# Attention with a banded bias: ScalarE writes the bias of three heads of four into PSUM, and the probability product moves between two score units

## What is computed

```python
scores = einsum('bhid,bhjd->bhij', q, k) * scale
diag = i - j
in_band = (diag >= 0) & (diag < 256)
scores = scores + where(in_band, learnable_bias[:, clip(diag, 0, 255)], 0)
scores = where(diag >= 0, scores, -inf)
m = maximum(max(scores, -1), off)
p = exp(scores - m)
out = einsum('bhij,bhjd->bhid', p, v) / (sum(p, -1) + exp(off - m))
x = layernorm(x + out @ Wo.T)
```

## Time and profile before

| | |
|---|---|
| three runs | 1764.86, 1770.17, 1771.36 us; median 1770.17 |
| the profiled execution | 1767.04 us, span on the core 1765.2 us |
| PE busy | 1640.3 us, 93% of the span |
| DVE busy | 1280.5 us, 73% |
| ACT busy | 1087.4 us, 62% |
| POOL busy | 212.0 us, 12% |
| identity matmuls L684 | 1280, 352.3 us busy |
| seeds L940 and zeros L938 on ACT | 320 and 128, 197.1 and 70.0 us busy |
| mean granted TensorE clock | 0.965 of full speed |

### The profile page before, as it was taken

One profiled execution on the slowest core, in us unless ns is written; L12 is line 12 of the kernel. 1 busy time (PEld: TensorE's weight loads), 2 busy tenths in 40 slices (PEclk: granted clock), 3 DMA queues, 4 the chain that ended last, 5 costly groups with the idle time before them and its releaser, 6 DMA issues. The chain is left out here.

```text
span 1765.2 us, 27891 instructions
## 1 busy us (share of the span) xinstructions
PE 1640.3 (93%) x9158; PEld 764.5 (43%) x9168; DVE 1280.5 (73%) x3812; ACT 1087.4 (62%) x1576; POOL 212.0 (12%) x109
## 2 busy tenths in 40 slices
PE   7999899889999999999999999999999998878773
PEld 3444344334444444444444444444444444433331
DVE  2454667568788888878888888888888872777776
ACT  2333233237877888787788878788887886333332
POOL 4323323230000000000000000000000000222222
PEclk9999999989999999999999999999999999989795
DMA  5447363534533633543452443335334120112211
GB/s 213 143 152 214 135 179 126 143 120 79 104 49 63 121 49 49 111 72 49 97 85 50 85 77 70 81 64 87 81 54 72 39 85 4 61 56 72 72 44 52
DMA packets 124501, 156.97 MB, mean 89 GB/s; under 512 B 14915, under 2 KB 80515, under 8 KB 124102
## 3 DMA queue, kind: packets, MB, share of 16 engines
q1 hardware_dynamic: 124358, 155.19, 38.1%
HBM read 103.90 MB, written 50.46 MB: 87 GB/s over the span
## 5 line engine op out<-in xcount | busy, mean ns | idle before, releaser
L925 ACT ACTIVATE probs<-ps 128x1024 f32<-128x1024 f32 (+3 forms) x768 | 592.3, 810 | 178.3 <-PE ps L684 119.3
L1165 DVE CUSTOM_DVE_ANT_0 junk<-ps,bias_q 128x384 bf16<-128x384 f32 (+2 forms) x1024 | 501.5, 502 | 137.3 <-PE ps L657 126.3
L657 PE MATMUL ps<-k_stack,q_stack 96*128 96x384 bf16 (+3 forms) x1536 | 492.8, 334 | 19.3 <-DVE mx L1165 12.0
L678 PE MATMUL ps<-q_stack,k_stack 99*128 99x512 bf16 (+3 forms) x1536 | 489.8, 328 | 18.7 <-ACT ps L940 10.4
L1158 DVE TENSOR_REDUCE mx<-ps 128x1 f32<-128x128 f32 (+3 forms) x768 | 365.2, 485 | 44.8 <-PE ps L657 37.1
L750 PE MATMUL ps<-attn 128*128 128x512 f32 x768 | 351.7, 602 | 10.5 <-DMA attn<-hT 9.3
L684 PE MATMUL ps<-bias_r,ident_r 128*128 128x384 f32 (+2 forms) x1280 | 352.3, 363 | 0.0
L699 PE MATMUL ps<-probs,v_sb 128*32 128x512 f32 (+3 forms) x3072 | 327.3, 498 | 0.1
L657 PEld LDWEIGHTS ps<-k_stack,q_stack 96*128 96x128 bf16 x1536 | 142.5, 97 | 373.9 <-DVE mx L1165 136.8
L684 PEld LDWEIGHTS ps<-bias_r,ident_r 128*128 128x128 f32 x1280 | 222.2, 192 | 36.9
L750 PEld LDWEIGHTS ps<-attn 128*128 128x128 f32 x768 | 144.9, 193 | 176.1 <-issue 163.7
(11 more groups left out here) (103 smaller groups left out, 1004.1 us busy)
## 6 DMA issues: line engine op xcount, KB each, us to landing
q_stack<-q_parts SPq DMA_DIRECT2D x192, 128.0 KB, 4.3
v_dram<-v_sb SPq DMA_DIRECT2D x32, 512.0 KB, 2.8
v_sb<-v_dram SPq DMA_DIRECT2D x32, 512.0 KB, 9.8
k_stack<-k_parts SPq DMA_DIRECT2D x32, 384.0 KB, 7.3
q_parts<-q_stack SPq DMA_DIRECT2D x84, 128.0 KB, 2.0
k_parts<-k_stack SPq DMA_DIRECT2D x84, 128.0 KB, 2.0
attn<-hT SPq DMA_DIRECT2D x8, 1024.0 KB, 7.0
k_stack<-k_parts SPq DMA_DIRECT2D x32, 256.0 KB, 8.0
```

Of the source, the lines that this page charges most:

```text
L657: pe.matmul(ps_ring[:, use.bank, 0:c1 - c0], q_stack[0:STACK, b, hl, I * P:(I + 1) * P], k_stack[0:STACK, b, hl, c0:c1], start=True, stop= ...
L678: mm = pe.matmul(ps_s[:, u % 2, hh, 0:w], k_stack[0:ROWS, b, hl, J * P:(J + 1) * P], q_stack[0:ROWS, b, hl, i0:i0 + w], start=not in_bank, ...
L925: act.activation(probs[:, (u // 2) % 3, 2 * pr:2 * pr + 2, 0:w], ps_s[:, pr, :, 0:w], ACT.Exp).then_inc(exp_done, 1)
L1165: ins = dve.tensor_tensor_reduce(out=junk[:, use.bank, 0:c1 - lo], in0=ps_ring[:, use.bank, lo - c0:c1 - c0], in1=bias_q[:, hl, BAND - t0 ...
```

## The change

In the tiles with a bias ScalarE now seeds the bank of head 1 as well, and only head 0 gets its bias from the identity matmuls. So there is a seed after every unit whose tile has a successor with a band, not only after the odd units: after an even unit for one head, after an odd unit for two. Every score unit of such a tile waits for its own seed. In TensorE's order `pv(T-1)` moves from the end of unit 2T+1 to the end of unit 2T, between the two units of tile T; the last product of the batch before moves from unit 1 to unit 0. ScalarE's copies stay after units 1 and 9. GpSimd's split follows the heads.

```diff
-PV_LEFT, EVAC_LEFT, OT_LEFT = 1, 1, 4
+PV_LEFT, EVAC_LEFT, OT_LEFT = 0, 1, 4
...
-        bias_s = sb("bias_s", [P, 2, 2, BAND])
-        bias_r = sb("bias_r", [P, 2, 2, 2, BAND], FP32R)
+        bias_s = sb("bias_s", [P, 2, 3, BAND])
+        bias_r = sb("bias_r", [P, 2, 2, 1, BAND], FP32R)
...
-                in_bank = bw and u % 2
-                if in_bank:
-                    pe.wait_ge(seeded, n * NBAND + BANDED.index(u // 2) + 1)
+                if bw:
+                    pe.wait_ge(seeded, 2 * (n * NBAND + BANDED.index(u // 2)) + u % 2 + 1)
                 for hh in range(2):
                     hl = 2 * (u % 2) + hh
+                    in_bank = bw and hl
...
                         if left and u == PV_LEFT:
                             pv(*before_in(g, b), n - 1, NT - 1)
-                        if u % 2 and u > 1:
+                        if u % 2 == 0 and u:
                             pv(g, b, n, u // 2 - 1)
...
-            def seed(g, T, done=0):
+            def seed(g, u, done=0):
...
+                pr = u % 2
+                heads = slice(1 - pr, 2)
+                nh = 1 + pr
+                if u < 2:
                     act.wait_ge(bias_split, 3 * (g + 1))
                 act.wait_ge(exp_done, FIRST + done)
                 act.sem_inc(act_passed, 1)
                 if w > bw:
-                    act.activation(ps_s[:, 1, :, bw:w], zero[:, :].unsqueeze(2).broadcast_to([P, 2, w - bw]),
-                                   ACT.Copy)
-                act.activation(ps_s[:, 1:2, :, 0:bw], bias_s[:, bass.ds(g % 2, 1), :, b0:b0 + bw], ACT.Copy)\
+                    act.activation(ps_s[:, pr, heads, bw:w],
+                                   zero[:, 0:nh].unsqueeze(2).broadcast_to([P, nh, w - bw]), ACT.Copy)
+                act.activation(ps_s[:, pr:pr + 1, heads, 0:bw],
+                               bias_s[:, bass.ds(g % 2, 1), pr:1 + 2 * pr, b0:b0 + bw], ACT.Copy)\
                     .then_inc(seeded, 1)
 
             def seed_after(g, n, u, more):
-                if u % 2 and u + 2 < NU:
+                if u + 2 < NU:
                     if u // 2 + 1 in BANDED:
-                        seed(g, u // 2 + 1, n * NU + u + 1)
-                elif u % 2 and more:
-                    seed(*more, 0, n * NU + u + 1)
+                        seed(g, u + 2, n * NU + u + 1)
+                elif more:
+                    seed(*more, u % 2, n * NU + u + 1)
...
             seed(0, 0)
+            seed(0, 1)
...
-                pool.tensor_copy(hi, bias_in[:, 0:2, ::-1]).then_inc(bias_split, 1)
+                pool.tensor_copy(hi, bias_in[:, 0:1, ::-1]).then_inc(bias_split, 1)
...
-                pool.tensor_tensor(lo, bias_in[:, 0:2, ::-1], hi.bitcast(FP32), ALU.subtract)\
+                pool.tensor_tensor(lo, bias_in[:, 0:1, ::-1], hi.bitcast(FP32), ALU.subtract)\
                     .then_inc(bias_split, 1)
-                pool.tensor_copy(bias_s[:, slot, :, :].rearrange("p a h c -> p (a h) c"), bias_in[:, 2:HG, ::-1])\
+                pool.tensor_copy(bias_s[:, slot, :, :].rearrange("p a h c -> p (a h) c"), bias_in[:, 1:HG, ::-1])\
                     .then_inc(bias_split, 1)
```

More of the change, by code:

```diff
@@ L926, in exp_unit @@
                                ACT.Exp).then_inc(exp_done, 1)
-            def seed(g, T, done=0):
-                c, J, i0, w = tile_cols(T)
-                b0, bw = band_cols(T)
-                if T == 0:
+            def seed(g, u, done=0):
+                c, J, i0, w = tile_cols(u // 2)
+                b0, bw = band_cols(u // 2)
+                pr = u % 2
+                heads = slice(1 - pr, 2)
+                nh = 1 + pr
+                if u < 2:
                     act.wait_ge(bias_split, 3 * (g + 1))
```

## The result

The changed kernel takes 1946.42 us (median of four runs, 1939.74 to 1949.37), against 1769.63 before: 1.0999 times as long, 95% interval 1.0962 to 1.1035. The forecast was 1925 in 1875 to 1975. The profiled execution took 1947.74 us, its span is 1945.9, 180.7 more than before.

What follows compares the result with a forecast made beforehand. TensorE seemed the limit before; afterwards ScalarE's 34.1 us list plus waits for TensorE make a batch 39.3 for 34.35 us. Over 31.3 batches that adds 155 to 1767.04, 1922; the median lies 3.1 higher: 1925, range 1875 to 1975.

Steps and rivals of the forecast that it cites:

- ScalarE's list: ScalarE's work per batch with no waits for TensorE: 34.1 us, 6.4 of it added by seeds, zeros and lost overlap.
- the lost overlap: Ten exponentials a batch now followed by a seed: 0.21 us each (0.11 waiting, 0.10 overlap lost), 2.1 together.
- The product of tile 0 and the copy: Units 0 to 3: product waits for ScalarE's copy, holding up unit 3's scores; exponential 3 at 6.12, a wait of 0.98.
- The same at tile 4: Units 10 and 11: product of tile 4 waits for the copy; exponential 11 at 18.05, a wait of 0.71 us.
- The product of tile 1: Units 3 to 5: product waits for exponential 3 to end; exponential 5 at 9.19, a wait of 0.71 us.
- The whole batch: Period from exponential 0 to the next batch's: 39.3 us for 34.35, 4.95 more.
- The busy shares: Profile sign per 100 us: ScalarE up to about 83, TensorE down to near 82.
- the rival with hidden waits: Moved product's three waits (2.4 us) vanish because ScalarE is late anyway: 36.9 us a batch, 1852 us; chance 0.11.
- The clock: Profile sign: granted clock of 1.00 in the attention, whose gaps are short with work between them.
- a rival in which the clock falls: TensorE, standing still 0.7 to 1.6 us several times a batch, drops to 0.80 clock: some 2000 us; chance 0.11.
- The sum of 155 us: Total added time: 4.95 us a batch over 31.3 batches, the first having no product left over.
- the pace of units 11 to 23: Unit 11 to batch end: ScalarE's list sets the pace, 20.97 us, with 0.3 left for exponential 22's wait.

Runs made afterwards that it cites:

- The seeds alone: Changed kernel with the product back in its old place behind the second unit, three-head seeds kept: 1863.85 us, 1.0564 times before.
- Short seeds: Changed kernel with head 1's seed writing 8 columns and no zeros, most of head 1's bias left out: 1872.52 us (single run).
- late seeds: Against the kernel with new seeds and the product in its old place: both seeds of a tile behind its second exponential; 1833.37 us (single run).
- the product alone: Seeds of before (heads 2 and 3), product moved between the units, copies after units 1 and 9: 1888.51 us, 1.0729 times before.

## Why the prediction was right, and what it left out

The direction and the size held, and the steps can be checked one by one against the batch at 1181.53 us.

- ScalarE's list. The new seeds and the lost overlap were sized to a few hundredths. In this batch ScalarE's exponential 1 comes after 1.55 us and its exponential 2 after 3.90; the forecast was 1.55 and 3.91.
- The product of tile 0 and the copy. Exponential 3 was forecast at 6.12 with a wait of 0.98; it comes at 6.01 with 0.81. The same at tile 4: exponential 11 was forecast at 18.05 with 0.71, and comes at 17.84 with 0.56.
- The product of tile 1. Exponential 5 was forecast at 9.19 with a wait of 0.71, and comes at 8.91 after the batch's start with 0.46.
- The whole batch. 39.3 was forecast, 38.98 measured without a fall of the clock. Up to exponential 5 it is 8.91 for 9.19, to exponential 10 6.53 for 6.40, to exponential 11 2.40 for 2.46, and from there to the end 21.14 for 21.27. The busy shares were forecast as 83 for ScalarE and 82 for TensorE; they are 81.1 and 85.2. The seeds alone, without the waits of the moved product, gave 37.08, where the rival with hidden waits said 36.9.
- The clock. Here the forecast was wrong by its own words: it said 1.00 in the attention, and gave 0.11 to a rival in which the clock falls. It does fall, but only at the stand-still in unit 2, for 3.4 us at a time and in 17 of 29 batches, at 1.5 us each. The rival's price (the clock of the last stage everywhere, 2000 us) was far too high, its chance too low. What failed was the sentence that the attention's gaps are short with work between them. The rule that I named ("TensorE: Matmul & The Clock Gate", The HAM clock gate, in the Trainium skill) pointed the right way: the slow level is the default, and only activity releases the full clock. This trace agrees: behind the stand-still the product takes up to 1.94 us, for 1.06.

The sum of 155 us against the span's 180.7: the 29 batches in the middle cost 135 where 144 were forecast. The falls in 17 of them cost 26. The first and the last two batches cost 16 where 11 were forecast; the last two have no maximum units, and took 29.4 us each before and 37.0 now. I read this as ScalarE's list felt in full where TensorE had been quick, and didn't test it. Outside the attention there are 3 us more. So the median came out 21 us above the forecast. The clock accounts for more than that. Without its falls the sum would have met the forecast almost exactly, but in part by luck: the batches in the middle were 9 us too high, and the ends and the other stages 8 too low.

Two reasons of the prediction need a limit. It gave ScalarE's list as the pace of units 11 to 23, and in the changed kernel that holds: from exponential 12 on no exponential of this batch shows a wait for TensorE. But the next limit lies close behind. Short seeds and late seeds give back only part of what they take off the list (2.0 of 3.2 us, 0.7 of 4), and with the late seeds ScalarE waits for score matmuls twice as long as with the seeds alone. And the moved product was charged mostly to the late copies. Alone it costs 3.95 us, and of these the copies make 1.4; of the other 2.5, 1.2 shows as longer waits of the products for exponentials, and the rest stays open.

## What to carry to other kernels

An engine that is idle 20% of the time may have no room for a chain's next link: add up its whole list with the lost overlaps, and compare it with the period, before giving it work from the engine that is full. A consumer that is moved ahead in an in-order queue brings its wait with it; name what it waits for, when that is made, and all that is queued behind. When the moved wait is longer than a microsecond on TensorE, look at the granted clock around it as well.

## What the runs showed of the hardware

- Behind a stand-still of TensorE of 1.4 us the granted clock was 0.52 for 3.4 us, and a product took up to 1.94 us instead of 1.06. It happened in 17 of 29 like batches of the changed kernel. What sets the others apart I can't show from these rows: their stand-still is as long (1.42 and 1.43).
- A lower share of work alone did not do it. At 87.0 and 87.6 of 100 us busy the clock was 1.00; with the stand-still it was 0.97 at 85.2 and 0.98 at 88.7. With the product alone (91.1 of 100), where the product waits up to 1.1 us for the same copy, it was 1.00 too.
- ScalarE starts a seed 0.11 us after the end of the exponential that it waits for the earlier trace rows (0.12 in the changed kernel, from 1182.53 to 1182.65), where two exponentials overlap by 0.10: a wait on its own result costs ScalarE 0.2 us, at each of ten new places a batch.
